# Perceiver layer on one core: norm scale in ScalarE's copy, film factors on GpSimd, kernel products on VectorE, another order of the preparation and of the late step

## The reference

```
x = x + cross(layernorm(x), ctx)      # 4 heads; top 32 of 257 scores; softmax; mean over heads
                                      #   film_in factors -> S4D convolution over 32 positions -> film_out factors
                                      #   + input, layernorm(g_ffn, b_ffn), gelu(.. @ W1 + b1) @ W2 + b2, layernorm
x = x + attn(layernorm(x))            # self-attention within 32 positions
x = x + ffn(layernorm(x))             # router: cosine to 8 centroids + linear; top 2 of 8 experts, each 256->128->256
```

## Time and profile before

| | before |
|---|---|
| median of 3 runs | 629.05 us |
| profiled execution, its time / its span | 635.15 / 633.4 us |
| TensorE matmul busy | 567.7 us (90%) |
| VectorE busy | 508.4 us (80%) |
| ScalarE busy | 291.6 us (46%) |
| GpSimd busy | 280.6 us (44%) |
| mean granted TensorE clock | 0.951 |

### The profile page before, as it was taken

One profiled execution on the slowest core, in us unless ns is written; L12 is line 12 of the kernel. 1 busy time (PEld: TensorE's weight loads), 2 busy tenths in 40 slices (PEclk: granted clock), 3 DMA queues, 4 the chain that ended last, 5 costly groups with the idle time before them and its releaser, 6 DMA issues.

```text
span 633.4 us, 12729 instructions
## 1 busy us (share of the span) xinstructions
PE 567.7 (90%) x4394; PEld 426.0 (67%) x4394; DVE 508.4 (80%) x1773; ACT 291.6 (46%) x750; POOL 280.6 (44%) x651
## 2 busy tenths in 40 slices
PE   2776697789999999999999999999999999998866
PEld 1535446376878687777777777868686868675755
DVE  6796367878989898989898989888898989976433
ACT  3110313346464646465546464545555554545522
POOL 4864202672535444444535353535353535252521
PEclk9996557999999999999999999999999999999988
DMA  7873030303030303040303030312111120000000
GB/s 180 323 258 142 0 114 2 115 2 107 18 108 8 118 2 124 2 124 2 124 1 119 6 97 29 84 42 71 54 56 70 34 91 10 1 10 2 9 1 17
DMA packets 16836, 42.38 MB, mean 67 GB/s; under 512 B 2722, under 2 KB 9458, under 8 KB 16260
## 3 DMA queue, kind: packets, MB, share of 16 engines
q1 hardware_dynamic: 16772, 41.57, 20.4%
HBM read 39.40 MB, written 2.16 MB: 66 GB/s over the span
## 4 chain that ended last, share of the span: by engine, by line
PE 67%; DVE 9%; issue 4%; ACT 2%; POOL 2%; POOLq 0%; DVEq 0%
PE BB L1104 9%; PE D L1104 9%; PE BB L1127 8%; PE SS L1092 4%; PE SS L1093 4%; PE D L1121 4%; DVE ang L809 3%; PE PC L1227 2%; PE PC L1229 2%; PE PC L1262 2%; PE BB L1187 2%; PE BB L1188 2%; PE BB L1221 2%; PE BB L1222 2%; PE SS L1079 2%
## 5 line engine op out<-in xcount | busy, mean ns | idle before, releaser
L521 POOL TENSOR_SCALAR var_in<-mv 128x1 f32<-128x1 f32 x64 | 13.9, 218 | 254.6 <-DVE mv L741 145.2
L776 DVE MATCH_REPLACE8 work<-top,work 128x257 f32<-128x257 f32 x192 | 77.3, 410 | 0.0
L1104 PE MATMUL D<-ang,e_w 128*128 128x128 f32 x512 | 72.3, 288 | 0.0
L1104 PEld LDWEIGHTS D<-ang,e_w 128*128 128x128 f32 x512 | 64.3, 198 | 10.1 <-issue 10.1
L770 DVE MAX8 top<-work 128x8 f32<-128x257 f32 x192 | 71.0, 411 | 0.0
L1121 PE MATMUL D<-expw,ang 128*128 128x256 f32 x256 | 64.7, 383 | 1.2 <-ACT ang L594 0.9
L1104 PE MATMUL BB<-ang,w 128*128 128x128 f32 x512 | 63.0, 283 | 0.9 <-ACT ang L589 0.9
L1104 PEld LDWEIGHTS BB<-ang,w 128*128 128x128 f32 x512 | 60.0, 196 | 4.0 <-issue 2.6
L1127 PE MATMUL BB<-expw,ang 128*128 128x256 f32 x256 | 57.9, 379 | 0.0
L615 ACT ACTIVATE expo<-SS,nmax,srs 128x257 f32<-128x257 f32 x64 | 32.7, 562 | 53.9 <-DVE work L756 53.7
L1121 PEld LDWEIGHTS D<-expw,ang 128*128 128x128 f32 x256 | 46.8, 190 | 9.5 <-DVE ang L809 1.9
(11 more groups left out here) (261 smaller groups left out, 1273.0 us busy)
## 6 DMA issues: line engine op xcount, KB each, us to landing
ctx_n<-in_ctx_n SPq DMA_DIRECT2D x16, 768.0 KB
ctx_t<-in_ctxT SPq DMA_DIRECT2D x16, 514.0 KB
ctx_t<-in_ctxT SPq DMA_DIRECT2D x16, 257.0 KB
xT<-in_xT SPq DMA_DIRECT2D x16, 128.0 KB, 2.3
x_all<-in_x SPq DMA_DIRECT2D x4, 512.0 KB, 12.7
out<-out_sb SPq DMA_DIRECT2D x16, 128.0 KB, 1.7
ctx_l<-in_ctx_l SPq DMA_DIRECT2D x16, 96.0 KB
w<-in_W SPq DMA_DIRECT2D x1, 1024.0 KB
```

Of the source, the lines that this page charges most:

```text
L776: V.match_replace(work[:, 2 * q + k, :], top[:, 2 * q + k, 8 * r8:8 * r8 + 8], work[:, 2 * q + k, :], TAKEN).then_inc(chains["taken"], 1)
L1104: ins = MM(bank[:, 128 * m:128 * m + 128], w[:, k, at:at + 128], xs[:, 128 * k:128 * k + 128], start=k == 0, stop=k == 1)
```

## The change

Scale and offset of the up-projection's norm are applied by ScalarE while it copies the transposed `hn` out of PSUM: one copy of 256 columns becomes two `Identity` activations of 128 columns with a scale and a bias per partition. The one-column products, the scaling of w1 and the addition to b1 go. The film products get the bias row as a product of one row, ScalarE copies all of them with the factor mod_gate, and GpSimd applies g_norm_in and b_norm_in (`film_inputs`, six tensor-tensor instructions). All four groups of kernel products are made by VectorE. The mask row is made by GpSimd and its scratch write stands ahead of the contexts in the DMA queue; contexts' natural layout has its own semaphore `ld_cn`. The kernel sums use banks B0 and B1, so that `keyed` of tile 1 stands before them. The centroids' norm moves into steps 1 and 2. In the late step the order changes on four engines.

```
@@ SyncE: preparation
             tokens(0)
-            contexts(Tile(0))
             load(c2[:, :, :], d["c2"], "ld_c")
             sp.wait_ge(s["setup_v"], 1)
             load(mask_dram.rearrange("a (b g) -> (a b) g", b=BT), vm[:, :], "scratch_out")
-            load(any_dram, anyv[:, 2:3], "scratch_out")
+            contexts(Tile(0))
...
+            load(wff[:, :, 0:2 * D], d["W_film_in"], "ld_film")
+            sp.wait_ge(s["scratch_out"], 16)
+            masks(Tile(0))
+            load(wff[:, :, 2 * D:4 * D], d["W_film_out"], "ld_film")
+            load(brow, d["b_film"], "ld_film")
+            load(awqk, d["awqk"], "ld_rows")
+            sp.wait_ge(s["any_v"], 1)
+            load(any_dram, anyv[:, 2:3], "scratch_any")
...
             rest(Tile(0))
@@ GpSimd: preparation
+            link(nc.gpsimd.tensor_copy(valid, vm8[:, :]))
+            ts(vm[:, :], valid, MASKED, -MASKED, ALU.mult, ALU.add).then_inc(s["setup_v"], 1)
...
-            tt(ang[:, 24:32, :], expw[:, 0:8, :], uu[:, 3, :].rearrange("p (o b) -> p o b", o=1).broadcast_to([128, 8, D]), ALU.mult).then_inc(s["prod_g"], 1)
...
+            def film_inputs():
+                pool.wait_ge(s["film_a"], 1)
+                pool.wait_ge(s["ld_rows"], LD_ROWS)
+                pool.wait_ge(s["setup_prod"], 4)
+                for f, n in ((film1, 128), (film2, 65)):
+                    link(tt(film_t[0:n, :], f[0:n, 0:D], bin_[0:n, :], ALU.mult))
+                    link(tt(f[0:n, D:2 * D], f[0:n, D:2 * D], film_t[0:n, :], ALU.add))
+                    ins = tt(f[0:n, 0:D], f[0:n, 0:D], gin[0:n, :], ALU.mult)
...
@@ GpSimd: step
                 if b:
                     norm(0, b)
-                    nc.gpsimd.tensor_tensor(xt_b[:, :], xt[:, :], b2[:, :], ALU.add).then_inc(s["xtb_g"], 1)
                 if c:
                     norm(3, c)
                     length(c)
                 if a:
                     weights(a, 0)
+                if a and a.n == 1:
+                    centroids()
+                if b:
+                    nc.gpsimd.tensor_tensor(xt_b[:, :], xt[:, :], b2[:, :], ALU.add).then_inc(s["xtb_g"], 1)
@@ ScalarE: step
                 if following:
                     query(following)
+                if b:
+                    A(ahead[:, :], b1[:, 0:1], ACT.Gelu)
                 if c:
                     wait(act, s["r_mm"], one(c))
                     A(r_c[:, :, :, :].rearrange("p j b t -> p b j t"), C0[:, D:2 * D].rearrange("p (b j t) -> p b j t", b=BT, j=2), ACT.Copy).then_inc(s["r_a"], 1)
                 if b:
-                    A(ahead[:, :], b1[:, 0:1], ACT.Gelu)
                     wait(act, s["hT_mm"], one(b))
-                    copy(hT[:, :], B0[:, 0:D], "hT_a")
+                    for k in range(2):
+                        ins = A(hT[:, 128 * k:128 * k + 128], B0[:, 128 * k:128 * k + 128], ACT.Identity, bias=bffn[:, k:k + 1], scale=gffn[:, k:k + 1])
+                    ins.then_inc(s["hT_a"], 1)
+                if b:
+                    gelus(act1, 0, B1, b1, "w1a_mm", "ga_a", b)
                 if following:
                     keyed(following)
                 if b:
-                    gelus(act1, 0, B1, b1, "w1a_mm", "ga_a", b)
                     gelus(act1, 1, B0, b1, "w1b_mm", "gb_a", b)
@@ VectorE: step
-                if a:
-                    take8(a, 0, 3)
                 if b:
                     wait(dve, s["rs0_g"], one(b))
                     V.tensor_scalar(hn[:, :], xt[:, :], mv[0][:, 0:1], rstd[0][:, 0:1], ALU.subtract, ALU.mult).then_inc(s["hn_v"], 1)
+                if a:
+                    take8(a, 0, 3)
@@ VectorE: preparation
-            products(1)
-            products(2)
...
+            for k in range(1, 4):
+                products(k)
@@ TensorE: step
+                if b:
+                    wait(pe, s["hn_v"], one(b))
+                    wait(pe, s["xt_v"], one(b))
+                    transposes(B0, hn, "hT_mm")
                 if c:
                     wait(pe, s["r_a"], one(c))
...
                     ins.then_inc(s["o2_mm"], 1)
                 if b:
-                    wait(pe, s["hn_v"], one(b))
-                    wait(pe, s["xt_v"], one(b))
-                    transposes(B0, hn, "hT_mm")
+                    wait(pe, s["hT_a"], one(b))
...
+                    wide(0, B1, w1, hT, "w1a_mm")
                 if following:
                     if c:
                         wait(pe, s["x2_v"], one(c))
                     keyed(following)
                 if b:
-                    wait(pe, s["hT_a"], one(b))
...
-                    wide(0, B1, w1, hT, "w1a_mm")
                     wide(1, B0, w1, hT, "w1b_mm")
```

More of the change, by code:

```diff
@@ L619, in step @@
                 following = next_tile(a)
+                if a and a.n == 1:
+                    act.wait_ge(s["kf_mm"], 1)
+                    copy(kern_f[:, :], D1[0:NF, 0:D], "kf_sb")
                 if dd:
@@ L630, in step @@
                     copy(amT[:, :, :].rearrange("p a b -> p (a b)"), PA[:, 0:256], "amT_a")
+                if a and a.n == 2:
+                    act.wait_ge(s["cent_t"], 1)
+                    A(route[:, :, NE:2 * NE], D0[:, 0:2 * NE].rearrange("p (a b) -> p a b", a=2), ACT.Copy).then_inc(s["route_a"], 1)
                 if a:
@@ L694, in _ @@
             query(Tile(1))
[L695 to L700 removed]
+            keyed(Tile(1))
             act.wait_ge(s["kt_mm"], 1)
[L702 to L705 removed]
+            copy(kern_t[:, :, :], BB[:, :, 0:D], "kt_sb")
             run(step)
@@ L987, in _ @@
             powers(4, 1, 5, 4, 8).then_inc(s["w8_v"], 1)
-            root_rows(0, 0, N_FIRST)
-            dve.wait_ge(s["srs_v"], 1)
-            maxima(first, 0)
-            take(first, 0)
             dve.wait_ge(s["ca"], 1)
@@ L1001, in _ @@
             link(V.scalar_tensor_tensor(u0[:, 1, :], o1[:, 1, :], -1.0, o2[:, 0, :], ALU.mult, ALU.subtract))
+            dve.wait_ge(s["setup_v"], 1)
+            link(V.reduce_max(anyv[:, 0:1], valid, AXX))
+            link(V.reciprocal(anyv[:, 1:2], anyv[:, 0:1]))
+            V.tensor_tensor(anyv[:, 2:3], anyv[:, 0:1], anyv[:, 1:2], ALU.mult).then_inc(s["any_v"], 1)
+            root_rows(0, 0, N_FIRST)
+            dve.wait_ge(s["srs_v"], 1)
+            maxima(first, 0)
+            take(first, 0)
             def products(k):
@@ L1135, in step @@
                     down(1)
+                if a and a.n == 2:
+                    pe.wait_ge(s["cent_n"], 1)
+                    pe.wait_ge(s["kf_sb"], 1)
+                    for k in range(2):
+                        ins = TR(D0[:, NE * k:NE * k + NE], cent[:, 128 * k:128 * k + 128], ident[0:NE, 0:NE])
+                    ins.then_inc(s["cent_t"], 1)
                 if dd:
+                    if dd.n == 0:
+                        pe.wait_ge(s["route_a"], 1)
                     wait(pe, s["xl3_v"], one(dd))
@@ L1144, in step @@
                     scores(a, 1)
+                if a and a.n == 1:
+                    pe.wait_ge(s["kt_sb"], 1)
+                    for h in range(2):
+                        for k in range(2):
+                            ins = MM(D1[0:NF, 128 * h:128 * h + 128], dft_k, kern_t[:, h, 128 * k:128 * k + 128], start=k == 0, stop=k == 1)
+                    ins.then_inc(s["kf_mm"], 1)
                 if dd:
@@ L1169, in step @@
                     wait(pe, s["amT_a"], one(b))
+                    wait(pe, ld_cn[b.p], b.half(N_CN, N_CN))
                     for k in range(BT):
```

194 lines of the change are left out of this document (76 added, 118 removed).

## The result

| | before | after |
|---|---|---|
| median on one chip | 629.26 us (4 runs, 628.9 to 631.32) | 605.89 us (4 runs, 605.33 to 607.18) |
| profiled execution, its time / its span | 635.15 / 633.4 us | 605.39 / 603.6 us |
| TensorE, VectorE, ScalarE, GpSimd busy | and the table before | 554.6, 498.1, 296.1, 280.7 us |
| mean granted TensorE clock | 0.951 | 0.980 |

The ratio is 0.9625 (95% interval 0.9598 to 0.9652): faster by 23.4 us. Forecast were 592.4 us (583 to 604); the measured time lies 1.9 us above the range and 13.5 above the forecast.

The account below looks back on a forecast made before the run. TensorE was taken to bound the steady steps, a chain over four engines the preparation and step 1. Gains of 21.6 + 2 + 10.8 + 2.3 = 36.7 us off the median 629.05 gave 592.4 us (583 to 604).

Parts of the forecast that it names:

- The last step of the sum: Whole kernel: 36.7 us won, subtracted from the runs' median 629.05 instead of the profiled 635.15, giving 592.4 instead of 598.5.
- Preparation: Before step 1: its first product (L1155) comes at 52.5 instead of 74.1 us, winning 21.6 us (18 to 23).
- VectorE's part: Preparation: three product groups at 2.3 us each end at 42.0 us, probabilities at 50.9, L1155 at 51.6 at the earliest.
- GpSimd's part: Preparation: `film_inputs`, six instructions of 0.72 us, ready near 47 us; row weights take 0.7 us after the probabilities.
- TensorE's own way: Preparation: film and wq*wk products end at about 40 us, `keyed` at about 44, L1155 at 51 (full clock) to 56 (half).
- Step 1: From L1155 to step 2's first score product, 35.2 us: 2 us less, bounds +1 and -7.
- 2.4 GHz through most of step 1: Rival on TensorE's clock in step 1: 5 us more won, 587.4 us; chance 0.15.
- Steady steps: Steps 3 to 14: waits for transposed probabilities, experts' sum and x2 go; 0.9 us each (0 to 1.1), 10.8 us in all.
- It fits, with 0.1 to 0.2 us to spare: Steady step: the two activations copying the transposes, together about 0.6 us after them, fit under the output projection of 0.87.
- The rival of the moved addition: Steady steps: moved L567 pushes L595 and L600 beside L784, VectorE's run 0.7 us longer, 600.8 us; chance 0.17.
- The ends: Steps 2, 15 and 16 win 0.6, 0.5 and 1.2 us, 2.3 in all.
- Identity: Rival: `Identity` with scale and bias needs its own table, two loads of 1.28 us per step, 633.4 us; chance 0.03.

Follow-up runs that it names:

- late back: The changed kernel with the late step's old order on all four engines, preparation and the two activations kept: 612.8 us, ratio 0.9671.
- norm alone: The kernel before with only the up-projection norm's scale and offset moved into ScalarE's copy, one-column products and w1 scaling gone: 622.22 us, ratio 0.982.
- without the bias: The changed kernel without the two one-row products that put b_film into the film products: 603.51 us, ratio 0.9532.
- one copy: The changed kernel with one plain copy of 256 columns for the two activations, leaving out that norm's scale and offset: 604.2 us.
- the two edits on top: The changed kernel with hT counted by halves, xt + b2 between third norm and lengths, and the qk_w copy ahead of film2's copies: 607.11 us, ratio 0.9631.

## Why the prediction was wrong

The direction, the kinds of gain and their order were right; the size was not.

**The last step of the sum failed: the subtraction from the median.** "That execution is 6.1 us above the median of the runs, 629.05, so I subtract from the median." The surplus was no noise that also the changed kernel would have. In the profiled execution VectorE lost the race between L914 and L567 in every steady step (0.82 us for L914), and winning it is one of the gains that I then counted at full size. The kernel before run again, at 627.07 close to the median, won it in all twelve steady steps: against that execution the twelve steps gain 2.5 us (32.17 to 31.96), not 7.1, and the whole pair differs by 21.7 us, near the 23.4 of the medians. The 24 steady steps of the two other kernels with the old late order (late back, norm alone) show the same two values and no other. Of the 8.1 us between the two executions the race is 4.6; step 1 and the last steps, where the granted clock differs, are the rest. That the unprofiled runs near 629 won the race is inferred, not seen. The unprofiled runs do not settle it: the kernel before lies at 628.9 to 631.3 us in the batch of the result, at 631.6 to 635.2 in the first batch of experiments, at 628.0 to 630.5 with two at 635.8 and 637.0 in the second, and at 627.8 and 631.1 to 635.4 in the third. From 635.15 the same sum gives 598.5, and 605.39 was measured.

**Preparation, 21.6 forecast, 18.2 measured.** VectorE's part held: the products took 2.26 each, as forecast, and ended at 41.0 (forecast 42.0), and the probabilities were there at 49.95 (50.9). GpSimd's part did not: `film_inputs` had to wait for ScalarE's copies of the film products, ended at 50.3 where I had 47, and two norm inputs of 1.2 us each stood in front of the row weights, which were ready at 54.3 and not at 51.6. Both are hidden behind TensorE's 55.88 (one group back on GpSimd changed nothing), and the failed step is TensorE's own way: "film and wq*wk products end at about 40 as before (two products more, a start 1 us earlier)". The start came 0.2 us earlier (29.35 beside 29.53), because tile 0's third scores waited 5.09 us for ScalarE, which itself had waited 8.49 us for VectorE. The two one-row products took 3.67 us, and the half clock lasted to 37.5 us (to 32.3 in the kernel before): the wq*wk product ended at 44.0, and `keyed` at 46.9 where I had 44. So the term that failed is the clock of this stretch. That is 2.9 of the 3.4 us missed; the 9.0 us from there to the first product lie between my 7 for full and 12 for half clock. In the changed kernel's second execution, with the full clock from 29.4 us, the wq*wk product ended at 40.1 and `keyed` at 43.0, as forecast. Leaving the two products out brought 2.1 us at `keyed` at nearly the same clock. Of the 18.2 the one-column products and the w1 scaling are some 8.4 (the part alone). The earlier mask row, which brought tile 0's scores from 20.36 to 15.30, did not bring the film products forward.

**Step 1, -2 forecast, -3.7 measured;** before's own step 1 differs by 2.3 us between executions (34.71 to 37.05). The granted clock was 1.00 from 60 to 70 us and 0.58 from 70 to 80: it fell at 71.6 us, inside the wait of 6.60 us before L1070. The rival "2.4 GHz through most of step 1" was half right.

**Steady steps, 0.9 forecast, 0.59 measured.** Both waits that come from L914 went, and so did that for x2. The failed step is "It fits, with 0.1 to 0.2 us to spare", said of the two activations under the output projection: they don't fit, by 0.19 us, and counting hT by halves, which takes the wait away, wins 0.22 per step. What I named as a sign of being wrong, a wait before the first half of the up-projection, is what the rows show. The remaining 0.1 is TensorE's own work, which I read too short: L1119 runs from 325.35 to 325.88, 0.53 us, and I counted 0.43.

**The rival of the moved addition** did not come about. GpSimd's L600, pushed behind L595, meets one VectorE instruction (0.94 us in place of 0.45):

```profile
341.82 0.45 DVE L813 SCALAR_TENSOR_TENSOR prob<-work,expo 128x257 f32<-128x257 f32 x1
342.20 0.94 DVE L813 SCALAR_TENSOR_TENSOR prob<-work,expo 128x257 f32<-128x257 f32 x1
...
341.26 0.73 POOL L595 TENSOR_TENSOR ang<-ang,rows 128x256 f32<-128x256 f32 x1
341.94 0.92 POOL L600 TENSOR_TENSOR out_sb<-ang 128x256 f32<-128x256 f32 x1
```

The 0.5 us are paid on VectorE, and TensorE has no wait there in steady steps. In the changed kernel a wait for the row weights shows only where fewer tiles are left, at step 16:

```profile
536.08 1.09 PE L1178 MATMUL PC<-prob,wsel 128*32 128x257 f32 x8 [1.65 <-POOL wsel L568]
```

There the row weights stand behind L595 and L600, 1.65 us in place of 0.5. **The ends,** forecast 2.3, gave 0.8: step 2 lost 0.4, step 15 lost 0.2, step 16 and what follows won 1.4. Why step 2 lost stays open. The 1.4 is not clear of noise: from there to the end the two other executions of the kernel before took 66.8 and 68.9 us, and the second execution of the changed kernel took 66.1. The Gelu table's load lies ahead of r_c as said.

**Identity** needed no table load of its own: none stands at L697 in any step.

## What to carry to other kernels

Before a gain is taken off a median, ask whether the profiled execution already contains the thing to be removed in its bad form; if it is a collision of two instructions that start within 0.07 us, one profile can't tell how often each outcome comes, and a second is cheap. Where two engines each have a chain to the same point, work out both ends to the same care: the products on VectorE were well understood and off the chain. If a copy is split in two, let the consumer count the halves.

## What was not expected of the hardware

- The race above: VectorE's 128x32 scaling and GpSimd's 128x256 addition, 0.05 to 0.07 us apart in the records, give 0.82 or 0.24 us for the former (0.72 to 0.73 or 0.76 to 0.77 for the latter). A strictly periodic program can repeat one outcome a dozen times, in either sense, and the other in the next execution. The Trainium skill (SBUF — State Buffer, Who interferes with whom) names `tensor_scalar` among the VectorE instructions that can take the ports shared with GpSimd, and says that the order of issue decides which engine blocks. The durations agree (0.82 beside 0.24 us for L914, which reads one tensor and one scalar per partition and so is no case of the two inputs named in the prediction). The order can't be read from the rows, in which L914 begins first both times. That the whole step then has two lengths is what these runs add.
- Step 2 of the changed kernel's variants took 31.4 to 31.7 us (both executions of the change, without the bias, with the old late order) or 36.6 to 36.7 (hT by halves, one copy, a group back on GpSimd). With hT by halves the granted clock was 0.68 from 90 to 100 us and 0.64 from 100 to 110:

```profile
100.00:110.00 10.00, 9.25 (x48) 4.91 (x46) 6.26 (x20) 2.23 (x6) 5.24 (x7) 0.64 0.01 2
```

In the changed kernel's first execution that window had a clock of 1.00. Steps 1 and 2 together were 64.4 to 65.5 us without such a dip and 68.7 to 69.2 with it (two kernels lie between, at 67.1 and 67.6). The times of one kernel go with the mean clock (with the two edits on top: 601.5 us at 0.982, 609.9 at 0.966), so several us of any single time here belong to it. What sets it off stays open.
